# Graph attention layer, one core: units of 128 edges, maxima by a scan, the one-hot transposed through one PSUM bank

## The chip, the cores and the metric

The kernel runs on 1 core of a Trainium2 chip. The metric is the device time of one execution in microseconds (us); what is given is the median of three runs.

## What is computed

One graph attention layer with a residual and a layer norm. There are 6250 nodes of 128 features and 206,250 edges (src, dst), among them one loop per node. Cut to what matters, with recv = src and send = dst, edges sorted by dst:

```python
wn_out = x[send] @ W_lin + b_lin
e_ij = leaky_relu(concat([x[recv], x[send]], -1) @ W_att + b_att, slope=0.2)
a_ij = (e_ij @ w_alpha)[:, 0]
a_exp = exp(a_ij - segment_max(a_ij, recv)[recv])
alpha = a_exp / max(segment_sum(a_exp, recv)[recv], 1e-12)
n_i = segment_sum(alpha[:, None] * wn_out, recv)
out = layernorm(x + elu(n_i))
```

## The kernel before

The nodes are cut into 49 blocks of 128 receivers. A first phase projects every node once: P (the receiver's half of the attention, kept in SBUF as three bf16 parts, `parts_mem`) and a row of 256 values for the sender (Q and V, written to the DRAM table `qv_table`). Meanwhile DVE sorts all edges by receiver block with a bitonic sort of 128 x 2048 keys; the transposes between its runs are PE's, and the copies out of PSUM are ACT's. Padding edges are made by counting (`make_padding`), so that every block fills whole units of `UNIT` = 256 edges. A chunk (`CHUNK`) is 512 edges, `PER` = 2 units; there are `NCH` = 427 chunks, enough for any input of this size.

The main loop runs over the chunks k, on every engine in an order that is written out by hand, with semaphores between the engines. For one chunk:

- ACT copies the senders' numbers (`stage_index`, L515), and POOL issues four indirect DMAs, each of which gathers 128 rows of the table (`gather`, L408 to L418) into one of `U` = 6 places of `rows`. A place is free once the sums of chunk k - 6 are done. After the last chunk four more are gathered (L421).
- DVE compares the lanes (the receivers' numbers within the block) with 0 to 127, which gives a one-hot (`make_onehot`, L954). PE transposes it (`turn_onehot`, L644) into one of two PSUM banks and ACT copies it to SBUF (`copy_onehotT`, L520).
- PE computes the hidden values (`hidden`, L652): per unit three bf16 matmuls of 256 columns, P's parts against the transposed one-hot, and per tile of 128 edges one fp32 matmul of the gathered rows with the identity (two passes each). The stationary operand of the bf16 ones is at an address from a register, the unit's block.
- ACT multiplies by the slope (`slope`, L526), DVE takes the maximum (`leaky_relu`, L961), and PE forms the scores of all 128 receivers for each edge, with a very low number where the receiver is another (`mask`, L670).
- DVE takes each unit's maximum (`lowest`, L975), then for each unit apart the block's new maximum, its growth, and its copy back (`new_peak`, `grow`, `set_peak`). ACT takes the exponential, one instruction per unit, and a factor by which the old sums shrink (`weigh`, L532).
- PE transposes the weights (`turn_weights`, L679), ACT copies them (`copy_weights`, L547), PE multiplies them with the gathered rows into one sum per unit (`chunk_sums`, L687), and DVE adds each unit's sum to its block's (`add_sums`, L1006).

What sets the order around the change is each engine's `step`, which does for several chunks at once:

```python
# PE, step k (L708)
turn_onehot(k + 4, j + 4); chunk_sums(k, j); turn_weights(k + 1, j + 1)
hidden(k + 4, ...); mask(k + 3, j + 3)
# DVE, step k (L1035), without the small operations
lowest(k + 2, j + 2); make_onehot(k + 5, j + 5); leaky_relu(k + 3, j + 3)
add_sums(k, j, 0, now); add_sums(k, j, 1, now)
# ACT, step k (L566)
slope(k + 3); copy_onehotT(k + 4); copy_weights(k + 1); weigh(k + 2); stage_index(k + U + 1)
```

A loop body holds `U` chunks (`chunks`, L295); at its start PE and DVE load the block numbers of its units into registers (`blocks_of`, L307). A tail divides the sums, applies ELU and the layer norm, and stores.

## Time and profile before

| | |
|---|---|
| median of the three runs | 3382.81 us (3382.03 to 3388.4) |
| profiled execution, span from first to last instruction | 2832.4 us |
| profiled execution, its own time | not listed; the median of the runs stands 550.4 us above the span |
| mean granted TensorE clock | 0.989 |
| DVE | 1889.7 us busy, 67%, 6126 instructions |
| ACT | 1479.4 us busy, 52%, 3418 instructions |
| DMA | 241.93 MB, mean 85 GB/s |

The span falls into three parts: sorting and projecting up to the first gather at 511.4 us, the main loop up to about 2779 us, and the tail of 53 us. The page's first part gives busy time by engine, the second the same in 40 slices of 70.8 us; the chain that ended last gives 26% to PE, 23% to DMA, 18% each to DVE and to "issue", 8% to POOL. Lines are lines of the kernel before; PEld is PE's weight load, and "rows<-qv_table,index" is the gather.

### The profile page before, as it was taken

Reading aid. Unit: us, or ns where it says so; the run is one execution under the profiler, and the core shown is the slowest. Engines: PE = TensorE matmul, PEld = TensorE weight load, DVE = VectorE, ACT = ScalarE, POOL = GpSimd, SP = SyncE. Lnnn points to the kernel's source line nnn. Section 1 sums busy time; section 2 is a strip of 40 time slices with the busy share of each in tenths; the row PEclk is TensorE's granted clock in tenths of the full one; section 3 lists DMA queues with packets and bytes.
Section 4 is the critical chain, followed back from the end, with each engine's and each line's share of the span. In section 5 each row is a group of like instructions: output and inputs, shape, how many; then the busy total and the mean of one; then the engine's idle time right before and its main releaser. Section 6 shows DMA issues by size and latency. Waiting matters only on the chain.

```text
span 2832.4 us, 60571 instructions
## 1 busy us (share of the span) xinstructions
PE 2139.7 (76%) x14416; PEld 1626.7 (57%) x14632; DVE 1889.7 (67%) x6126; ACT 1479.4 (52%) x3418; POOL 1725.1 (61%) x1739
## 2 busy tenths in 40 slices
PE   4981111588888888888888888888888888888872
PEld 1321111466666666666666666666766666666651
DVE  7969999666666666666666666666666666666546
ACT  3781111355555555555555555555555555555544
POOL 0000000677777777777777777777777777777760
PEclk9999999999999999999999999999999999999996
DMA  3110000233333333333333333333333333333493
GB/s 98 41 36 2 0 0 0 75 103 100 102 100 101 101 102 101 101 101 101 101 100 101 102 100 102 100 101 101 101 100 100 102 100 101 101 101 101 96 79 63
DMA packets 99135, 241.93 MB, mean 85 GB/s; under 512 B 29041, under 2 KB 42057, under 8 KB 98907
## 3 DMA queue, kind: packets, MB, share of 16 engines
q0 software_dynamic: 82816, 226.19, 29.7%
q1 hardware_dynamic: 16298, 15.51, 1.9%
q8 instruction: 6, 0.10, 0.0%
q14 instruction: 15, 0.12, 0.0%
HBM read 231.91 MB, written 9.68 MB: 85 GB/s over the span
## 4 chain that ended last, share of the span: by engine, by line
PE 26%; DMA 23%; issue 18%; DVE 18%; POOL 8%; DVEq 3%; ACT 3%; SPq 0%; POOLq 0%; ACTq 0%
DMA rows<-qv_table,index 22%; PE hidden_ps L666 9%; POOL rows L415 8%; PE masked_ps L677 8%; DVE keys_i L844 3%; DVE keys_i L843 3%; PE hidden_ps L611 3%; PE hidden_ps L661 3%; PE hidden_ps L610 2%; DVE new_low L990 2%; ACT index L518 1%; DVE onehot L957 1%; DVE leaky L965 1%; DVE growth L998 1%; DVE sums L1013 1%
## 5 line engine op out<-in xcount | busy, mean ns | idle before, releaser
L415 POOL DMA_INDIRECT rows<-qv_table,index x1724 | 1716.7, 996 | 590.1 <-issue 398.8
L980 DVE TENSOR_REDUCE unit_low<-masked_ps 128x2 f32<-128x512 f32 x429 | 296.8, 692 | 797.7 <-PE masked_ps L677 797.7
L666 PE MATMUL hidden_ps<-identf,rows 128*128 128x128 f32 x3448 | 571.8, 289 | 317.7 <-DMA rows<-qv_table,index 317.7
L666 PEld LDWEIGHTS hidden_ps<-identf,rows 128*128 128x128 f32 x3448 | 454.2, 192 | 440.1 <-DMA rows<-qv_table,index 434.9
L693 PE MATMUL turned_ps<-rows,weights 128*128 128x129 f32 x3416 | 475.2, 282 | 0.5 <-ACT weights L551 0.5
L539 ACT ACTIVATE weightsT<-masked_ps,new_low 128x256 f32<-128x256 f32 x858 | 403.8, 471 | 93.3 <-DVE new_low L990 92.2
L677 PE MATMUL masked_ps<-leaky,w_cols 128*128 128x512 f32 x860 | 442.3, 596 | 11.6 <-issue 0.4
L551 ACT ACTIVATE weights<-turned_ps 128x512 f32<-128x512 f32 x428 | 255.5, 597 | 339.2 <-PE turned_ps L684 339.2
L661 PE MATMUL hidden_ps<-onehotT,parts_mem 128*128 128x256 bf16 x2586 | 425.1, 274 | 3.2 <-ACT onehotT L524 3.2
L693 PEld LDWEIGHTS turned_ps<-rows,weights 128*128 128x128 f32 x3416 | 416.2, 192 | 0.6 <-ACT weights L551 0.6
L524 ACT ACTIVATE onehotT<-turned_ps 128x512 bf16<-128x512 bf16 x431 | 257.4, 597 | 304.4 <-PE turned_ps L649 303.8
L530 ACT ACTIVATE sloped<-hidden_ps 128x512 f32<-128x512 f32 x430 | 256.4, 596 | 225.0 <-PE hidden_ps L666 223.3
L1013 DVE SCALAR_TENSOR_TENSOR sums<-sums,shrink,turned_ps 128x129 f32 x854 | 296.0, 347 | 50.1 <-DVE sums L1013 0.2
L965 DVE TENSOR_TENSOR leaky<-hidden_ps,sloped 128x512 f32<-128x512 f32 x430 | 297.4, 692 | 7.0 <-ACT sloped L530 6.9
L649 PEld LDWEIGHTS turned_ps<-identb,onehot 128*128 128x128 bf16 x1724 | 133.1, 98 | 282.7 <-issue 246.0
L957 DVE TENSOR_TENSOR onehot<-lane,lanes 128x512 bf16<-128x512 bf16 x432 | 294.4, 682 | 0.7 <-DVE lanes L948 0.7
L661 PEld LDWEIGHTS hidden_ps<-onehotT,parts_mem 128*128 x2586 | 254.6, 98 | 24.4 <-issue 4.1
L684 PE MATMUL turned_ps<-identf,weightsT 128*128 128x128 f32 x1712 | 256.9, 273 | 0.0
L640 PE MATMUL turned_ps<-identf,keys_i 128*128 128x128 f32 x208 | 51.2, 427 | 230.7 <-DVE keys_i L844 194.1
L684 PEld LDWEIGHTS turned_ps<-identf,weightsT 128*128 128x128 f32 x1712 | 200.7, 141 | 0.5 <-issue 0.5
L649 PE MATMUL turned_ps<-identb,onehot 128*128 128x128 bf16 x1724 | 167.6, 220 | 35.9 <-DVE onehot L957 35.9
L640 PEld LDWEIGHTS turned_ps<-identf,keys_i 128*128 128x128 f32 x208 | 40.8, 223 | 240.9 <-DVE keys_i L844 165.1
(123 smaller groups left out, 1984.9 us busy)
## 6 DMA issues: line engine op xcount, KB each, us to landing
rows<-qv_table,index POOLq DMA_INDIRECT x1724
qv_table<-qv_out SPq DMA_DIRECT2D x49, 128.0 KB, 1.7
out<-x_sb SPq DMA_DIRECT2D x2, 1344.0 KB
keys_i<-in_src SPq DMA_DIRECT2D x1, 768.0 KB
keys_i<-in_dst SPq DMA_DIRECT2D x1, 768.0 KB
recv<-in_src SPq DMA_DIRECT2D x1, 604.5 KB
out<-x_sb SPq DMA_DIRECT2D x1, 256.0 KB
recv<-in_src SPq DMA_DIRECT2D x1, 195.2 KB
```

Of the source, the lines that this page charges most:

```text
L415: g.indirect_dma_start(out=rows[:, j, c, 0:2 * F], out_offset=None, in_=table, in_offset=bass.IndirectOffsetOnAxis(ap=index[:, j, c:c + 1] ...
L539: last = a.activation(weightsT[:, j % 2, unit], masked_ps[:, j % 2, unit], ACT.Exp, bias=new_low[:, j % 2, i:i + 1])
L649: mm = t.transpose(onehotT_ps[:, j % 2, c * P:(c + 1) * P], onehot[:, j % 2, c, :], identb[:])
L661: t.matmul(whole[:, unit], p_parts[:, bass.ds(of[i], 1), s, :].rearrange("p a f -> p (a f)"), onehotT[:, j % 3, unit], start=(s == 0), sto ...
L666: mm = t.matmul(whole[:, c * P:(c + 1) * P], rows[:, j % U, c, 0:F], identf[:], start=False, stop=(c == (i + 1) * UC - 1), skip_group_chec ...
L677: t.matmul(whole, w_cols[:], leaky[:, j % 2, :], start=False, stop=True).then_inc(masked_done, 1)
L684: mm = t.transpose(weights_ps[:, c * P:(c + 1) * P], weightsT[:, j % 2, c * P:(c + 1) * P], identf[:])
L693: mm = t.matmul(unit_sums_ps[:, c // UC, :], weights[:, j % 2, c * P:(c + 1) * P], rows[:, j % U, c, F:R], start=(c % UC == 0), stop=(c % ...
L957: v.tensor_tensor(onehot[:, j % 2], lane[:].unsqueeze(1).to_broadcast([P, C, P]), lanes[:, bass.ds(k * C, C)].unsqueeze(2).to_broadcast([P ...
L965: v.tensor_tensor(leaky[:, j % 2, :], hidden_ps[:, j % 2, :], sloped[:, j % 2, :], ALU.max).then_inc(leaky_ready, 1)
L980: v.tensor_reduce(unit_low[:], masked_ps[:, j % 2, :].rearrange("p (i e) -> p i e", i=PER), AX_X, ALU.max, negate=True).then_inc(unit_low_ ...
L1013: v.scalar_tensor_tensor(out=at, in0=at, scalar=shrink[:, j % 2, i:i + 1], in1=unit_sums_ps[:, i, :], op0=ALU.mult, op1=ALU.add).then_inc( ...
```

## The change

- `UNIT` is 128 edges (`PER` = 4), so a chunk holds four units, one per tile; with less padding `NCH` is 415. Nothing is gathered after the last chunk, and no step issues work for a chunk past it (`real`).
- The ring of gathered rows has 8 places (`U`); a loop body holds 8 chunks and loads block numbers every 4 (`HALF`).
- The running maxima of a chunk's units come from one scan: a table `fresh` (made once, in the sort) holds a high number where a unit is the first of its block, and `peaks` keeps the maximum after every unit. Growth is one subtraction per chunk.
- In `hidden` the gathered rows are transposed (one pass) ahead of P's parts, which are matmuls of 128 columns; the wait for the gather is the first of the stage.
- The transposed one-hot has one PSUM bank in place of two, and four places in SBUF. PE transposes it for chunk k + 5 in step k. The bank gained goes to the sums, which have one region per unit.
- ACT's step is ordered anew; the exponentials are of 128 columns.
- Lanes and senders stay in the sorted layout and are read with a stride. The sort has one more stage. Several buffers share memory.

```diff
-    PER = 2
+    PER = 4
...
-    SLOTS = 8
+    SLOTS = 14
     AHEAD = 4
-    U = 6
+    U = 8
+    HALF = U // 2
...
+    assert BODIES * U + AHEAD < NCH
...
-        onehotT_ps = turned_ps[:, 0:2 * CHUNK].bitcast(BF16).rearrange("p (s c) -> p s c", s=2)
-        weights_ps = turned_ps[:, 2 * CHUNK:3 * CHUNK]
-        sums_ps = turned_ps[:, 3 * CHUNK:4 * CHUNK]
+        onehotT_ps = turned_ps[:, 0:CHUNK].bitcast(BF16)
+        weights_ps = turned_ps[:, CHUNK:2 * CHUNK]
+        unit_sums_ps = turned_ps[:, 2 * CHUNK:4 * CHUNK].rearrange("p (i c) -> p i c", i=PER)[:, :, 0:F + 1]
...
             chunks(pool, gather)
-            for k in range(NCH, NCH + AHEAD):
-                gather(k // U, k % U)
...
             def weigh(k, j):
...
+                act.wait_ge(new_low_ready, k + 1)
                 for i in range(PER):
                     unit = slice(i * UNIT, (i + 1) * UNIT)
-                    act.wait_ge(new_low_ready, k * PER + i + 1)
                     last = a.activation(weightsT[:, j % 2, unit], masked_ps[:, j % 2, unit], ACT.Exp,
-                                        bias=new_low[:, j % 2, i:i + 1])
+                                        bias=peaks[:, bass.ds(k * PER + i + 1, 1)])
...
             def step(i, j):
                 k = i * U + j
-                slope(k + 3, j + 3)
-                copy_onehotT(k + 4, j + 4)
-                copy_weights(k + 1, j + 1)
-                weigh(k + 2, j + 2)
-                stage_index(k + U + 1, (j + 1) % U, i + 1 + (j + 1) // U)
+                if real(k + 5):
+                    copy_onehotT(k + 5, j + 5)
+                if real(k + 2):
+                    weigh(k + 2, j + 2)
+                if real(k + 1):
+                    copy_weights(k + 1, j + 1)
+                if real(k + 4):
+                    slope(k + 4, j + 4)
+                if real(k + U + 1):
+                    stage_index(i, j + U + 1)
...
             def turn_onehot(k, j):
                 pe.wait_ge(onehot_ready, k + 1)
-                if past(k, 2):
-                    pe.wait_ge(onehotT_ready, k - 1)
+                if past(k, 1):
+                    pe.wait_ge(onehotT_ready, k)
...
             def hidden(k, j, rounds, of):
                 pe.wait_ge(onehotT_ready, k + 1)
                 if past(k, 2):
                     pe.wait_ge(leaky_ready, k - 1)
+                pe.wait_ge(gathered[j % U], rounds * (16 * C))
                 whole = hidden_ps[:, j % 2, :]
                 for i in range(PER):
                     unit = slice(i * UNIT, (i + 1) * UNIT)
+                    t.matmul(whole[:, unit], rows[:, j % U, i, 0:F], identf[:], is_transpose=True,
+                             start=True, stop=False, skip_group_check=True)
                     for s in range(3):
-                        t.matmul(whole[:, unit], p_parts[:, bass.ds(of[i], 1), s, :].rearrange("p a f -> p (a f)"),
-                                 onehotT[:, j % 3, unit], start=(s == 0), stop=False, skip_group_check=True)
-                    if i == 0:
-                        pe.wait_ge(gathered[j % U], rounds * (16 * C))
-                    for c in range(i * UC, (i + 1) * UC):
-                        mm = t.matmul(whole[:, c * P:(c + 1) * P], rows[:, j % U, c, 0:F], identf[:],
-                                      start=False, stop=(c == (i + 1) * UC - 1), skip_group_check=True)
+                        mm = t.matmul(whole[:, unit], p_parts[:, bass.ds(of[i], 1), s, :].rearrange("p a f -> p (a f)"),
+                                      onehotT[:, j % 4, unit], start=False, stop=(s == 2), skip_group_check=True)
...
             def step(i, j, ahead):
                 k = i * U + j
-                turn_onehot(k + 4, j + 4)
+                if real(k + 5):
+                    turn_onehot(k + 5, j + 5)
                 chunk_sums(k, j)
-                turn_weights(k + 1, j + 1)
-                hidden(k + 4, j + 4, i + 1 + (j + 4) // U, ahead[j * PER:(j + 1) * PER])
-                mask(k + 3, j + 3)
+                if real(k + 1):
+                    turn_weights(k + 1, j + 1)
+                if real(k + 4):
+                    hidden(k + 4, j + 4, i + 1 + (j + 4) // U, ahead)
+                if real(k + 3):
+                    mask(k + 3, j + 3)
...
+            def new_peaks(k, j):
+                dve.wait_ge(unit_low_ready, k + 1)
+                if past(k, 1):
+                    dve.wait_ge(new_low_ready, k)
+                v.tensor_tensor_scan(peaks[:, bass.ds(k * PER + 1, PER)], fresh[:, bass.ds(k * PER, PER)], unit_low[:],
+                                     peaks[:, bass.ds(k * PER, 1)], ALU.max, ALU.min).then_inc(new_low_ready, 1)
...
             def step(i, j, of):
                 k = i * U + j
-                lowest(k + 2, j + 2)
-                make_onehot(k + 5, j + 5)
...
-                leaky_relu(k + 3, j + 3)
...
+                if real(k + 2):
+                    lowest(k + 2, j + 2)
+                    new_peaks(k + 2, j + 2)
+                if real(k + 5):
+                    make_onehot(i, j + 5)
+                if real(k + 3):
+                    leaky_relu(k + 3, j + 3)
+                if real(k + 2):
+                    old_peaks(k + 2, j + 2)
+                    mark_ones(i, j + 2)
+                    grow(k + 2, j + 2)
+                for n in range(PER):
+                    add_sums(k, j, n, of)
```

How the change moves instructions, at three places. First, PE at the start of the main loop's lead-in. `onehot` is what DVE made, `turned_ps` the PSUM it is transposed into; before:

```order
L310 TENSOR_LOAD blocks [waits w_cols_ready,split,blk_loaded]
L649 MATMUL turned_ps<-identb,onehot 128x128 [waits onehot_ready]
L649 MATMUL turned_ps<-identb,onehot 128x128 x3
L661 ISA [waits onehotT_ready]
L661 MATMUL hidden_ps<-onehotT,parts_mem 128x256
```

and now:

```order
L297 TENSOR_LOAD blocks [waits w_cols_ready,split,blk_loaded]
L646 MATMUL turned_ps<-identb,onehot 128x128 [waits onehot_ready]
L646 MATMUL turned_ps<-identb,onehot 128x128 x3
L646 MATMUL turned_ps<-identb,onehot 128x128 [waits onehotT_ready,onehot_ready]
L646 MATMUL turned_ps<-identb,onehot 128x128 x3
L658 MATMUL hidden_ps<-identf,rows 128x128 [waits gathered0,onehotT_ready]
```

One transpose of four tiles more stands ahead of the first hidden stage: PE is one one-hot further on than before, and stays so in the loop.

Second, DVE's step for one chunk in the loop. `unit_low` are the units' maxima (negated), `low_peak` or `peaks` the running ones; before:

```order
L980 TENSOR_REDUCE unit_low<-masked_ps 128x2 [waits new_low_ready,masked_done]
L957 TENSOR_TENSOR onehot<-lane,lanes 128x512 [waits onehotT_done]
L990 ISA [waits peak_ready,weightsT_ready,unit_low_ready]
L990 TENSOR_TENSOR new_low<-unit_low,low_peak 128x1
L972 TENSOR_SCALAR rows<-lanes 128x4 [waits chunk_sums_done]
L998 TENSOR_TENSOR growth<-new_low,low_peak 128x1 [waits shrink_ready,new_low_ready]
L965 TENSOR_TENSOR leaky<-hidden_ps,sloped 128x512 [waits masked_done,sloped_ready]
```

and now:

```order
L986 TENSOR_REDUCE unit_low<-masked_ps 128x4 [waits new_low_ready,masked_done]
L994 SCALAR_TENSOR_TENSOR peaks<-fresh,peaks,unit_low 128x4 [waits new_low_ready,unit_low_ready]
L961 TENSOR_TENSOR onehot<-lane,lanes 128x512 [waits onehotT_done]
L969 TENSOR_TENSOR leaky<-hidden_ps,keys_i 128x512 [waits masked_done,sloped_ready]
L1002 TENSOR_TENSOR old_low<-peaks,fresh 128x4 [waits growth_ready,new_low_ready]
```

The one-hot stands behind the reduction as before, and now behind the scan as well, which waits for the reduction.

Third, PE's step in the loop, from the weights' transposes into the hidden stage; before:

```order
L684 MATMUL turned_ps<-identf,weightsT 128x128 [waits weights_ready,weightsT_ready]
L684 MATMUL turned_ps<-identf,weightsT 128x128 x3
L661 ISA [waits leaky_ready,onehotT_ready]
L661 MATMUL hidden_ps<-onehotT,parts_mem 128x256
L661 ISA
L661 MATMUL hidden_ps<-onehotT,parts_mem 128x256
```

and now:

```order
L679 MATMUL turned_ps<-identf,keys_i 128x128 [waits weights_ready,weightsT_ready]
L679 MATMUL turned_ps<-identf,keys_i 128x128 x3
L658 MATMUL hidden_ps<-identf,rows 128x128 [waits gathered5,leaky_ready,onehotT_ready]
L661 ISA
L661 MATMUL hidden_ps<-onehotT,parts_mem 128x128
```

The wait for the gather moved ahead of P's matmuls. Each of these, an ISA row (a register computation) and a matmul, is half as wide and comes twelve times per chunk in place of six.

## Rows read from the trace of the kernel before

**Rows 1.** The page, parts 1 and 2: busy time; busy tenths of POOL in 40 slices.

```profile
PE 2139.7 (76%) x14416; PEld 1626.7 (57%) x14632; DVE 1889.7 (67%) x6126; ACT 1479.4 (52%) x3418; POOL 1725.1 (61%) x1739
...
POOL 0000000677777777777777777777777777777760
```

**Rows 2.** All instructions of line 415, POOL's gathers, and what its idle time ended with.

```profile
L415 POOL DMA_INDIRECT rows<-qv_table,index x1724: 942/946/2342, 511.4 to 2768.4; - x192
...
  issue: 398.8, 1273
```

**Rows 3.** The timeline of POOL: start, us, instruction, [idle before, releaser].

```profile
1202.48 0.95 POOL L415 DMA_INDIRECT rows<-qv_table,index  x1 [0.30 <-issue]
1203.73 1.32 POOL L415 DMA_INDIRECT rows<-qv_table,index  x1 [0.30 <-issue]
1205.36 0.94 POOL L415 DMA_INDIRECT rows<-qv_table,index  x1 [0.31 <-issue]
```

**Rows 4.** Two stretches: length, busy us (instructions) of each engine, granted clock, DMA.

```profile
540.00:2660.00 2120.00, 1822.13 (x13263) 1449.22 (x13466) 1317.19 (x4893) 1212.67 (x2857) 1623.19 (x1632) 1.00 0.35 101
2660.00:2769.00 109.00, 81.41 (x560) 64.33 (x568) 55.76 (x208) 50.35 (x120) 70.12 (x73) 0.95 0.84 82
```

**Rows 5.** The timeline of PE over one chunk.

```profile
1201.57 0.38 PE L676 MATMUL masked_ps<-onehotT,other 128*128 128x512 bf16 x1
1201.79 1.02 PE L677 MATMUL masked_ps<-leaky,w_cols 128*128 128x512 f32 x2
1202.65 0.39 PE L649 MATMUL turned_ps<-identb,onehot 128*128 128x128 bf16 x4
1202.87 1.11 PE L693 MATMUL turned_ps<-rows,weights 128*128 128x129 f32 x8
1203.82 0.60 PE L684 MATMUL turned_ps<-identf,weightsT 128*128 128x128 f32 x4
1204.25 0.49 PE L661 MATMUL hidden_ps<-onehotT,parts_mem 128*128 128x256 bf16 x3
1205.30 0.71 PE L666 MATMUL hidden_ps<-identf,rows 128*128 128x128 f32 x4 [0.56 <-DMA rows<-qv_table,index]
```

**Rows 6.** The timeline of DVE over the same chunk.

```profile
1202.94 0.69 DVE L980 TENSOR_REDUCE unit_low<-masked_ps 128x2 f32<-128x512 f32 x1 [1.99 <-PE masked_ps L677]
1203.55 0.68 DVE L957 TENSOR_TENSOR onehot<-lane,lanes 128x512 bf16<-128x512 bf16 x1
```

**Rows 7.** The timeline of all engines where the pipeline fills.

```profile
520.24 1.29 DVE L957 TENSOR_TENSOR onehot<-lane,lanes 128x512 bf16<-128x512 bf16 x2 [0.68 <-DVE lanes L948]
...
520.99 0.61 PE L649 MATMUL turned_ps<-identb,onehot 128*128 128x128 bf16 x4 [35.94 <-DVE onehot L957]
...
529.96 0.68 DVE L980 TENSOR_REDUCE unit_low<-masked_ps 128x2 f32<-128x512 f32 x1
...
530.78 0.16 DVE L990 TENSOR_TENSOR new_low<-unit_low,low_peak 128x1 f32<-128x1 f32 x1
```

**Rows 8.** The updates of the sums (line 1013) and DVE's register loads (line 310).

```profile
L1013 DVE SCALAR_TENSOR_TENSOR sums<-sums,shrink,turned_ps x854: 341/348/353, 540.5 to 2778.9; 128x129 f32 x171
...
L310 DVEq TENSOR_LOAD <-blocks x73: 597/1101/1128, 519.6 to 2771.0; - x73
```

**Rows 9.** PE after its longest wait of the even stretch, and the clock granted behind it.

```profile
1975.72 0.71 PE L666 MATMUL hidden_ps<-identf,rows 128*128 128x128 f32 x4 [2.03 <-DMA rows<-qv_table,index]
...
1977.20:1980.40 3.20, 2.98 (x11) 1.89 (x11) 0.91 (x2) 1.18 (x2) 2.45 (x3) 0.50 0.44 123
```

**Rows 10.** The timeline of DVE: the last stage of the sort.

```profile
507.50 1.23 DVE L843 TENSOR_TENSOR keys_i<-keys_i 128x1024 f32<-128x1024 f32 x1
508.64 1.22 DVE L844 TENSOR_TENSOR keys_i<-keys_i 128x1024 f32<-128x1024 f32 x1
```

More of the change, by code:

```diff
@@ L675, in mask @@
                 whole = masked_ps[:, j % 2, :]
-                t.matmul(whole, other[:], onehotT[:, j % 3, :], start=True, stop=False)
+                t.matmul(whole, other[:], onehotT[:, j % 4, :], start=True, stop=False)
                 t.matmul(whole, w_cols[:], leaky[:, j % 2, :], start=False, stop=True).then_inc(masked_done, 1)
@@ L1046, in step @@
-                new_peak(k + 2, j + 2, 1, later)
-                add_sums(k, j, 1, now)
-                grow(k + 2, j + 2, 1, later)
-                set_peak(k + 2, j + 2, 1, later)
-            chunks(dve, step, lambda i: blocks_of(mybir.EngineType.DVE, i, 0, U + 2))
+                if real(k + 2):
[5 more added lines that the diff above has]
+                    leaky_relu(k + 3, j + 3)
```

233 lines of the change are left out of this document (116 added, 117 removed).

## Prediction

> **What bounds the kernel now.** The page first [rows 1]: PE is the busiest engine (76%), POOL is at 61% and gathers from slice 8 to slice 38 without a break; no engine is full. A busy share cannot choose between them, so the next view is POOL's own line. The 1724 gathers are four for each chunk of 512 edges (427 chunks and 4 after them), 0.946 us in the median, and nearly all of POOL's idle time is put down to "issue" or to a releaser of a moment ago [rows 2]. The timeline shows why: each gather starts 0.30 us after the end of the one before, whatever the releaser's name, and now and then one takes 1.32 us in place of 0.95, beside the one-hot comparison on DVE, which starts 0.18 us before it [rows 3, 6]. So a chunk costs POOL 4 x 0.946 + 4 x 0.305 + about 0.2 = 5.2 us, and POOL never truly waits. In the long even stretch it was busy 1623 of 2120 us, with 1632 gathers: 1.30 us for each, 5.20 us a chunk, at full TensorE clock [rows 4]. The others follow it: PE stands before the matmuls that use gathered rows (the row at 1205.30) [rows 5], DVE waits 1.99 us before the reduction over the masked scores [rows 6]. **POOL's gathers are the bound, and PE and DVE each have about a microsecond of slack per chunk.** After the last edge the chunks hold nothing but padding; in 2660 to 2769 us 73 gathers take 109 us, 1.49 us each [rows 4].
>
> **What goes with fewer chunks.** 427 + 4 gathered chunks become 415 with none after them. If POOL stayed the bound, 16 chunks at 5.2 us would go, 83 us.
>
> **What the PE work of a chunk becomes.** Differences of starts give what the work holds PE for [rows 5]: four bf16 transposes of the one-hot 0.22 us (1202.65 to 1202.87), the eight passes of the sums 0.95, four fp32 transposes of the weights 0.43, the bf16 mask 0.22, and the fp32 mask matmuls 1.02 to their end. In the hidden stage the eight fp32 passes of the gathered rows become four transposes, priced like those of the weights: 0.43. Six matmuls of 256 columns become twelve of 128. Their nearest row at 128 bf16 columns is the one-hot's, four weight loads with four matmuls in 0.22 us, 0.055 each: 0.67 us. The bound on the other side is the 256-column row, 0.49 us for three with 0.16 of it tail, so 0.11 each: 1.32. I take 0.055, because load, type and columns are the same, and keep the other end. From the first one-hot transpose to the end of the mask: 0.22 + 0.95 + 0.43 + 0.43 + 0.67 + 0.22 + 1.02 = **3.94 us**. PE has less work than before.
>
> The Trainium skill, TensorE: Matmul & The Clock Gate, section Back-to-back issue gap, says that a sustained stream of weight load and matmul pairs runs at about 81 ns a pair for 128 columns. The row of this trace says 55 ns for four pairs; by the page's figure an estimate for the twelve is 1.0 us in place of 0.67.
>
> **The step in which the slack goes.** In the loop before, PE's step k transposes one-hot k+4, and DVE's step k makes one-hot k+5: it lies ready a whole step ahead. After, PE's step k starts with the transposes of one-hot k+5, and DVE still makes k+5 in its step k. DVE makes it behind the reduction and the scan for chunk k+2, and the reduction waits for the mask of k+2, which is the last work of PE's step k-1. So nothing overlaps on this path: PE's whole step, then reduction, scan, one-hot, then PE's whole next step. That circle bounds the chunk, whatever the engines' busy shares are:
> - end of the mask to the start of the reduction: 1201.79 + 1.02 to 1202.94, 0.13 us [rows 5, 6]; the floor is 0.04;
> - reduction 0.69 [rows 6];
> - hand-over to an instruction that needs it at once: 529.96 + 0.68 to 530.78, 0.14 [rows 7];
> - the scan over four columns, which the trace does not show: between the 0.16 us of the one-column minimum [rows 7] and 0.3; I take 0.16, since its four columns are far nearer to one than to the hundreds of a long operation;
> - one-hot 0.68 [rows 6], and to PE's first transpose 520.24 + 0.69 to 520.99, 0.06 [rows 7]. DVE may prepare the one-hot during the scan, so no further gap;
> - PE's step 3.94.
>
> Sum: 0.13 + 0.69 + 0.14 + 0.16 + 0.68 + 0.06 + 3.94 = **5.80 us**, above POOL's 5.20. POOL gets ahead until its ring of eight is full, then waits.
>
> **What else can lie on it.** DVE's four updates of the sums (0.348 us each) [rows 8] take the place of two. Each waits for the one before; with the 0.14 hand-over they need 1.96 us. They start once the sums' matmuls end, 0.22 + 1.11 us into PE's step, and end at about 3.3, before the mask does at 3.94: covered, by 0.6 us. The block numbers are loaded into registers every four chunks in place of six, 1.10 us on DVE's sequencer [rows 8]. The load begins once the last update is handed over, near 3.0, and ends near 4.1, about when the next reduction may start: 0 to 0.4 us late in one chunk of four; I take 0.05 a chunk. The three small operations per unit (minimum, growth, copy) become two per chunk: they hung on nothing and save nothing now. ACT's two exponentials of 256 columns become four of 128; ACT was busy 1213 of 2120 us [rows 4], 2.97 a chunk, and stays under 4: covered by the circle's 5.8, and also worth nothing if POOL is the bound. But its order matters: it now copies the weights after the shrink factor, which waits for the updates; 3.3 + 0.2 + 0.6 = 4.1 us, needed at 3.94 + 1.86 + 0.22 = 6.0. Covered.
>
> **TensorE's clock.** PE now stands still for the circle's DVE part, 1.86 us, in every chunk. In the long stretch before, where PE paused for less, the clock was granted in full [rows 4]; but after one wait of 2.03 us for a gather it was granted at 0.50, the 1.2 GHz level, in 1977.2 to 1980.4 us [rows 9]. Work on PE takes twice as long there, so such a fall costs about half of these 3.2 us. With pauses nearly as long as that wait in every chunk, I take one fall in eleven chunks, 0.15 a chunk; its ends are 0 and the rival below. Together 5.80 + 0.05 + 0.15 = **6.0 us a chunk**.
>
> **The sum.** The updates ran from 540.5 to 2778.9 us [rows 8], with the last one's end 2779.3. After: 410 full steps at 6.0 = 2460; the last five issue no hidden stage, about 3.7 each, 18. The sorting phase gets one more stage over 2048 keys, 2.4 us [rows 10], a table of 1792 columns in three operations, at those rows' price 2 us each, and loses wider padding and a strided unpacking; I take +1, between -6 and +6. So the last update ends at 540.5 + 1 + 2460 + 18 = 3019.5, 240 us later. The 53 us behind it stay. The profiled execution has a span of 2832.4 us; the median of the runs is 3382.8, and the 550.4 us between them are in no view. I keep them constant: 2832.4 + 240 = 3072 in the profile, and **3382.8 + 240 = 3623 us**. Low end of this case: 5.6 a chunk (all hand-overs at their floors, no load, no fall), 3459. High end: 6.5, 3828.
>
> **Rivals.**
> - *The short matmul pairs are slow.* Each of the twelve is preceded by a register computation; if pairs with one run at 0.08 to 0.11 us, the circle grows by 0.3 to 0.66 us: 410 of these are 123 to 271 us, **3746 to 3894**. For it: the 256-column rows never show a shorter pace, as they can't. 
> - *The clock falls regularly.* If the 1.86 us pause takes the clock to 1.2 GHz in every second chunk, at 1.6 us each, a chunk costs 0.65 us more than forecast, 267 us in 410: **3890**, and twice that if it does so in every chunk. For it: [rows 9]. Against: PE is busy for two thirds of the chunk. Chance 0.12.
> - *POOL stays the bound*, the side of faster. Its place is the gather, its price 5.2 us a chunk, and it decides once the circle is shorter than POOL's period. Then 83 us go, **3300**. This needs the circle 0.6 us shorter than its own rows; or a gather that is dearer in the timed runs than in the profile: if the 550 us outside the span lay in the 1724 gathers, 0.32 us each, POOL's period would be 6.5 and cover the circle's 6.0, and 16 chunks fewer would save 100 us. Nothing in the trace speaks for it. Chance 0.12.
> - *The one-hot is not on a circle*, because some step ahead hides it: the order of both engines, with one more transpose in PE's lead-in but as many one-hots in DVE's, excludes it. It would end as the rival before; its chance is in there.
>
> **How the numbers follow.** Forecast 0.58, slow pairs 0.18, clock 0.12, POOL 0.12. The time is the forecast's, 3623. The range takes in the forecast's ends and the slow pairs: 3450 to 3900; outside are POOL's case and the worse half of the clock's. A change of 0.2%, 7 us, is about what a measurement of this kernel can tell from none. Faster 0.12, within it 0.02 (the POOL case with a circle just over it), slower 0.86.
>
> **What would show it.** In the profile after: gathers with idle time before them that ends with the sums' matmuls; DVE's one-hot followed within 0.1 us by PE's transposes, which wait on it each chunk; the reduction waiting for the mask, less than 4 us of PE work between; a chunk period of 5.7 to 6.4; the twelve pairs in about 0.7 us. It is wrong if the gathers still follow each other at 1.30 us, if one-hots lie ready before PE asks, or if the span grows by less than 75 us; if the span goes as said and the time does not, what lies outside the span was no constant.

## The result, and the profile after

| | median of the runs |
|---|---|
| before | 3382.42 us (3378.69 to 3388.4, 4 runs) |
| after | 3647.11 us (3634.74 to 3658.77, 4 runs; granted clock 0.814 to 0.855) |

The ratio is 1.0787, 95% interval 1.0758 to 1.0816: slower by 264.7 us, where 3623 (+240) was predicted. The kernel before takes about 3382 us in some sessions on a chip and 2834 in others (both on one and the same chip, ten minutes apart), and the rows ahead of the prediction come from an execution of the second kind, while the measured ratio comes from the first. So each ratio below is taken to the kernel before of its own session. What differs between the sessions is a subject of the experiments.

The profiled execution of the changed kernel took 3643.12 us with a span of 3641.1: 2 us apart, not 550. Its page, first and second part:

```profile
span 3641.1 us, 65506 instructions
...
PE 2307.6 (63%) x14980; PEld 1770.6 (49%) x14981; DVE 2113.6 (58%) x5544; ACT 1417.7 (39%) x4145; POOL 1608.8 (44%) x1675
...
POOL 0000034555555554555555555555555555555550
PEclk9985557888888887888888888888888887888886
```

POOL, which had no real pause before [rows 1], is down to 44%, and the mean granted clock is near 0.8 in nearly every slice of the loop. The gathers and the updates of the sums, each from the view of its line (count, duration min/median/max, first and last start), and the longest waits of the kernel (us in total, times, longest):

```profile
L408 POOL DMA_INDIRECT rows<-qv_table,index x1660: 943/949/2057, 515.4 to 3549.1; - x185
...
L1020 DVE SCALAR_TENSOR_TENSOR sums<-sums,shrink,turned_ps x1660: 348/349/353, 571.5 to 3587.8; 128x129 f32 x185
```

```profile
POOL rows L408 <- PE turned_ps L688: 924.6, 332, 14.8
...
PE turned_ps L646 <- DVE onehot L961: 751.6, 303, 34.0
...
DVE unit_low L986 <- PE masked_ps L672: 433.5, 340, 3.0
```

A gather costs what it did [rows 2], but now POOL waits for its ring (L688 are the sums' matmuls). PE waits for the one-hot, and DVE for the mask: the circle of the prediction, with its names. From the first update to the last it is 3016.3 us for 415 chunks, 7.27 each. The timeline of two chunks, PE and the three DVE operations of the circle (start, duration, in brackets the idle time before and who ended it):

```profile
1501.33 0.44 PE L646 MATMUL turned_ps<-identb,onehot 128*128 128x128 bf16 x4 [2.13 <-DVE onehot L961]
1501.86 1.15 PE L688 MATMUL turned_ps<-rows,keys_i 128*128 128x129 f32 x8
1502.85 0.60 PE L679 MATMUL turned_ps<-identf,keys_i 128*128 128x128 f32 x4
1503.28 0.27 PE L658 MATMUL hidden_ps<-identf,rows 128*128 128x128 f32 x1
1503.39 0.33 PE L661 MATMUL hidden_ps<-onehotT,parts_mem 128*128 128x128 bf16 x3
1503.56 0.28 PE L658 MATMUL hidden_ps<-identf,rows 128*128 128x128 f32 x1
...
1504.63 1.02 PE L672 MATMUL masked_ps<-leaky,w_cols 128*128 128x512 f32 x2
1505.68 0.69 DVE L986 TENSOR_REDUCE unit_low<-masked_ps 128x4 f32<-128x512 f32 x1 [0.70 <-PE masked_ps L672]
1506.63 0.23 DVE L994 TENSOR_TENSOR_SCAN peaks<-fresh,peaks,unit_low 128x4 f32 x1 [0.26 <-issue]
1506.85 0.69 DVE L961 TENSOR_TENSOR onehot<-lane,lanes 128x512 bf16<-128x512 bf16 x1
1507.59 0.40 PE L646 MATMUL turned_ps<-identb,onehot 128*128 128x128 bf16 x4 [1.95 <-issue]
1507.83 1.96 PE L688 MATMUL turned_ps<-rows,keys_i 128*128 128x129 f32 x8
1509.58 1.06 PE L679 MATMUL turned_ps<-identf,keys_i 128*128 128x128 f32 x4
```

PE does the work of the first chunk at full clock, 6.26 us from transpose to transpose. In the second the same eight passes of the sums take 1.96 us in place of 1.15 and the transposes 1.06 in place of 0.60: the 1.2 GHz level, after a pause of 1.95 us. The next L646 starts at 1515.17, 7.58 us later.

Taking the differences between the starts of successive one-hot transposes over the whole loop, 134 chunks hold no time at the low level, with a median of 5.94 us; 278 hold some, with a median of 7.58. (The ends of the mask show where the difference lies: the median from the one-hot's transpose to there, PE's step, is 3.99 us in the first kind and 5.63 in the second.) By windows the granted clock is even (PE, PEld, DVE, ACT and POOL busy with counts, then clock, DMA share, GB/s); 273 gathers in 500 us are 7.33 us a chunk:

```profile
1500.00:2000.00 500.00, 351.72 (x2387) 282.35 (x2388) 265.99 (x754) 198.87 (x613) 263.00 (x273) 0.83 0.25 72
```

### The profile page after: what moved, and what is told of

Read it like the earlier page. It is cut to its first block, busy times and chain, and to the rows that moved or that the text cites. A ratio compares the mean times of both kernels' runs of the same rounds, so it can differ in the third digit from the quotient of the medians.

```text
span 3641.1 us, 65506 instructions
## 1 busy us (share of the span) xinstructions
PE 2307.6 (63%) x14980; PEld 1770.6 (49%) x14981; DVE 2113.6 (58%) x5544; ACT 1417.7 (39%) x4145; POOL 1608.8 (44%) x1675
## 4 chain that ended last, share of the span: by engine, by line
PE 54%; DVE 22%; issue 14%; DVEq 4%; another core or an unknown queue 3%; ACT 1%; DMA 1%; SPq 0%; ACTq 0%
PE turned_ps L688 16%; PE masked_ps L672 8%; PE hidden_ps L661 8%; PE turned_ps L679 6%; DVE onehot L961 6%; PE hidden_ps L658 5%; DVE unit_low L986 5%; PE turned_ps L646 5%; DVE sums L1020 3%; DVE keys_i L854 3%; DVE keys_i L853 3%; PE hidden_ps L608 2%; PE masked_ps L671 2%; PE hidden_ps L607 2%
## 5 line engine op out<-in xcount | busy, mean ns | idle before, releaser
L408 POOL DMA_INDIRECT rows<-qv_table,index x1660 | 1600.4, 964 | 1486.0 <-PE turned_ps L688 924.6
L1020 DVE SCALAR_TENSOR_TENSOR sums<-sums,shrink,turned_ps 128x129 f32 x1660 | 580.2, 350 | 702.8 <-PE turned_ps L688 489.5
L646 PE MATMUL turned_ps<-identb,onehot 128*128 128x128 bf16 x1660 | 184.1, 240 | 969.3 <-DVE onehot L961 751.6
L646 PEld LDWEIGHTS turned_ps<-identb,onehot 128*128 128x128 bf16 x1660 | 104.0, 103 | 1311.2 <-DVE onehot L961 809.5
L986 DVE TENSOR_REDUCE unit_low<-masked_ps 128x4 f32<-128x512 f32 x415 | 287.0, 692 | 613.9 <-PE masked_ps L672 433.5
L688 PE MATMUL turned_ps<-rows,keys_i 128*128 128x129 f32 x3320 | 627.4, 348 | 8.4 <-ACT keys_i L539 6.4
L661 PE MATMUL hidden_ps<-onehotT,parts_mem 128*128 128x128 bf16 x4980 | 617.9, 250 | 0.3 <-issue 0.3
L688 PEld LDWEIGHTS turned_ps<-rows,keys_i 128*128 128x128 f32 x3320 | 540.7, 246 | 20.4 <-ACT keys_i L539 11.0
L661 PEld LDWEIGHTS hidden_ps<-onehotT,parts_mem 128*128 x4980 | 519.5, 119 | 51.9
L527 ACT ACTIVATE keys_i<-masked_ps,peaks 128x128 f32<-128x128 f32 x1660 | 472.1, 375 | 2.7 <-DVE peaks L994 2.7
L679 PE MATMUL turned_ps<-identf,keys_i 128*128 128x128 f32 x1660 | 356.7, 356 | 0.0
L969 DVE TENSOR_TENSOR leaky<-hidden_ps,keys_i 128x512 f32<-128x512 f32 x415 | 283.7, 684 | 35.6 <-issue 34.2
L679 PEld LDWEIGHTS turned_ps<-identf,keys_i 128*128 128x128 f32 x1660 | 289.0, 191 | 1.1 <-issue 0.6
L637 PE MATMUL turned_ps<-identf,keys_i 128*128 128x128 f32 x208 | 50.3, 422 | 231.7 <-DVE keys_i L854 195.1
```

The costliest lines, as they stand in the source:

```text
L408: g.indirect_dma_start(out=rows[:, j, c, 0:2 * F], out_offset=None, in_=table, in_offset=bass.IndirectOffsetOnAxis(ap=index[:, j, c:c + 1] ...
L527: last = a.activation(weightsT[:, j % 2, unit], masked_ps[:, j % 2, unit], ACT.Exp, bias=peaks[:, bass.ds(k * PER + i + 1, 1)])
L646: mm = t.transpose(onehotT_ps[:, c * P:(c + 1) * P], onehot[:, j % 2, c, :], identb[:])
L661: mm = t.matmul(whole[:, unit], p_parts[:, bass.ds(of[i], 1), s, :].rearrange("p a f -> p (a f)"), onehotT[:, j % 4, unit], start=False, s ...
L679: mm = t.transpose(weights_ps[:, c * P:(c + 1) * P], weightsT[:, j % 2, c * P:(c + 1) * P], identf[:])
L688: mm = t.matmul(unit_sums_ps[:, c, :], weights[:, j % 2, c * P:(c + 1) * P], rows[:, j % U, c, F:R], start=True, stop=True)
```

## The experiments

### First session: what costs the changed kernel its time, and the kernel before again

e1 is the kernel before, unchanged.

> The kernel before, unchanged, to see its span and granted clock in every run. The changed kernel's span lies 2 us under its time, so the 550 us between time and span of the kernel before are no constant. Theory A (its timed runs run in another regime than its one profiled execution: the short pauses of TensorE at the gathered rows let the clock fall, as they did once in the trace): time near 3382 us, span near 3380, granted clock 0.80 to 0.90. Theory B (something outside the span of this kernel alone): span near 2832, clock 0.99, time near 3382.

Measured: 3384.32 us, ratio 1.0005 (0.9995 to 1.0015), span 3384.1. The span is as long as the time, so the 550 us are inside it: the first update starts 14 us later than in the rows ahead of the prediction (554.2 against 540.5), and from the first update to the last it is 2776 us in place of 2238. **538 of the 550 us are in the main loop.** That is the outcome that theory A expected; its cause, the clock, is another matter. The window of 1500 to 2500 us, and its longest waits:

```profile
1500.00:2500.00 1000.00, 764.47 (x5091) 606.12 (x5089) 497.76 (x1848) 422.54 (x1077) 603.28 (x615) 0.88 0.28 81
```

```profile
DVE unit_low L980 <- remote: 669.2, 103, 7.8
...
ACT weights L551 <- remote: 509.0, 178, 7.9
...
ACT sloped L530 <- remote: 355.7, 100, 10.9
```

615 gathers in 1000 us: 6.50 us a chunk, not 5.2 [rows 4]. ACT's L551 copies the weights and L530 multiplies by the slope. "Remote" is what the profile says when no instruction on the core ended close to the release. One such place in the timeline, PE, ACT and DVE:

```profile
1505.62 0.60 PE L684 MATMUL turned_ps<-identf,weightsT 128*128 128x128 f32 x4
...
1507.82 1.02 PE L677 MATMUL masked_ps<-leaky,w_cols 128*128 128x512 f32 x2
1508.67 0.39 PE L649 MATMUL turned_ps<-identb,onehot 128*128 128x128 bf16 x4
...
1511.01 0.60 ACT L551 ACTIVATE weights<-turned_ps 128x512 f32<-128x512 f32 x1 [5.29 <-remote]
...
1511.74 1.15 PE L693 MATMUL turned_ps<-rows,weights 128*128 128x129 f32 x8 [2.68 <-issue]
...
1515.34 0.60 ACT L530 ACTIVATE sloped<-hidden_ps 128x512 f32<-128x512 f32 x1 [2.81 <-remote]
1515.48 0.69 DVE L980 TENSOR_REDUCE unit_low<-masked_ps 128x2 f32<-128x512 f32 x1 [7.40 <-remote]
```

ACT's copy L551 waits for the transposes L684, which are over at 1506.2, and starts at 1511.01. DVE's reduction waits for the mask L677, over at 1508.84, and starts at 1515.48. The trace's records of the semaphores agree: the signals of L684 and L677 are there at 1510.98 and 1515.37. **PE's completion signals come late**. Long waits like these two are met about once in 26 us (103 for DVE's reduction), but smaller delays are common: in the loop the signal of L684 comes more than 0.5 us after the end of its matmul in 296 of its 424 records, the latest by 7.7 us. Signals of DVE and ACT follow the end of their instruction within 0.02 us wherever they are recorded. In the trace ahead of the prediction no signal of PE in the loop is late by more than 0.02 us. Between the long waits PE runs chunk after chunk in 4.23 us, so POOL's bound of 5.2 is undershot and then given back.

The changed kernel has them too, but in its loop they are fewer (the hidden stage's signal is over 0.5 us late in 40 of 414 records). One ahead of it is long. Where the pipeline fills and gathers follow each other without a pause, the hidden stage's last matmul ends at 531.59 and its signal stands at 555.88, and all wait for it:

```profile
531.07 0.53 PE L661 MATMUL hidden_ps<-onehotT,parts_mem 128*128 128x128 bf16 x3
...
555.91 0.60 ACT L518 ACTIVATE keys_i<-hidden_ps 128x512 f32<-128x512 f32 x1 [26.77 <-remote]
```

e2 takes the one-hot off the circle: DVE makes it one chunk earlier.

```diff
             make_onehot(0, 0)
+            make_onehot(0, 1)
             for k in range(4):
-                make_onehot(0, k + 1)
+                make_onehot(0, k + 2)
...
-                if real(k + 5):
-                    make_onehot(i, j + 5)
+                if real(k + 6):
+                    make_onehot(i, j + 6)
```

> The changed kernel, but DVE makes one-hot k+6 in step k (and one more in its lead-in), so that it lies ready a step before PE transposes it. Theory A (the circle of PE's whole step with reduction, scan and one-hot bounds the chunk, and the pause in it lets the clock fall): the circle is broken, POOL's 5.2 us bound again, 541 + 415 x 5.25 + 53 = 2770 us, at most 2900, clock over 0.97. Theory B (DVE's longer step with four updates is the bound by itself): 5.8 to 6.3 us a chunk, 3000 to 3200 us. Theory C (the regime of the clock is what the kernel before suffers too): 3200 to 3400 us.

Measured: 3352.74 us, ratio 0.9903 (0.9883 to 0.9923). That is 8% below the changed kernel and 1% below the kernel before, so **the one-hot's place is what made the change slower than the kernel before**. But the 2770 us expected of theory A were missed by far, and the time is in the range of theory C, where both kernels suffer from the same thing. The loop stays at 6.6 us a chunk:

```profile
1500.00:2500.00 1000.00, 747.15 (x5287) 561.71 (x5288) 581.27 (x1663) 438.71 (x1363) 592.54 (x606) 0.86 0.28 79
```

Chunks without low clock take 5.23 us here, POOL's period; those with it take 8.16, and the late signals are here too:

```profile
DVE unit_low L986 <- remote: 592.7, 112, 6.9
```

e3 leaves the one-hot for k + 5 but puts it first in DVE's step:

```diff
+                if real(k + 5):
+                    make_onehot(i, j + 5)
                 if real(k + 2):
                     lowest(k + 2, j + 2)
                     new_peaks(k + 2, j + 2)
-                if real(k + 5):
-                    make_onehot(i, j + 5)
```

> The changed kernel, but DVE makes one-hot k+5 at the start of its step, ahead of the reduction and the scan. Theory A: PE can start its step after DVE's last update and a 0.7 us one-hot, while the reduction still waits for nothing but the mask; the one-hot is off the circle, 5.2 to 5.5 us a chunk, 2750 to 2880 us if the clock stays up. Theory B (DVE's work is the bound): no better than 6 us a chunk, 3080 us.

Measured: 3419.68 us, ratio 1.0104 (1.0085 to 1.0124). The two swapped blocks are worth 227 us. The expected 2750 to 2880 were missed as in e2: the 203 chunks without low clock have a median of 5.09 us, as theory A said, but those with it 6.84, and the mean is 6.8.

e4 fills PE's pause in the changed kernel with matmuls that nobody reads, after the mask:

```diff
+            def idle_work(k, n):
+                pe.wait_ge(onehotT_ready, k)
+                for _ in range(n):
+                    t.matmul(turned_ps[:, 256:256 + P], identb[:], identb[:], start=True, stop=True)
...
                     mask(k + 3, j + 3)
+                if real(k + 5):
+                    idle_work(k + 6, 16)
```

> The changed kernel with 16 small matmuls after the mask, identity against identity into unused columns of the one-hot's bank, about 0.9 us of work in PE's pause of 1.9 us; nothing waits for them. Their result is read by nobody. Theory A (1.03 of the 7.33 us of a chunk are the clock, which falls because of the pause): the clock stays over 0.97 and the chunk takes the circle's 6.26 us: 541 + 410 x 6.26 + 18 + 53 = 3180 us. Rival (the pause is not what lowers the clock): clock near 0.82 and time 3640 us or more.

Measured: 3513.9 us, ratio 1.0392 (1.0365 to 1.042): 133 us less, with more work on PE and the same circle.

```profile
1500.00:2500.00 1000.00, 762.64 (x7327) 638.41 (x7328) 553.19 (x1579) 417.20 (x1288) 562.31 (x572) 0.93 0.26 75
```

The clock is at 0.93 in place of 0.83. The time at the low level between 600 and 3300 us fell from 870 to 365 us. So PE's own pause lets the clock fall, and the fall costs time. The expected 3180 was missed by far: PE is still 1 us idle after the filler, 137 chunks still hold low clock, and the late signals have become more (that of the one-hot's transposes is over 0.5 us late in 249 of 387 records, in the changed kernel in none of the 249 that are recorded).

### Second session: where the late signals come from

e5 puts the same 16 matmuls into e2, e8 puts them into the kernel before, after its mask. e7 leaves out two of P's three parts in e2's hidden stage (`for s in range(1)`). In e6 three of a chunk's four gathers are left out. The scaled exponential and the larger divisor only keep the numbers bounded, since most gathered rows are then stale and the output means nothing:

```diff
-                for c in range(C):
+                for c in range(1 if past(k, U) else C):
                     g.indirect_dma_start(
...
-                    act.wait_ge(gathered[r], rounds * (16 * C))
+                    act.wait_ge(gathered[r], rounds * 16 + 48)
...
-                a.activation(shrink[:, j % 2, :], growth[:, j % 2, :], ACT.Exp).then_inc(shrink_ready, 1)
+                a.activation(shrink[:, j % 2, :], growth[:, j % 2, :], ACT.Exp, scale=0.0).then_inc(shrink_ready, 1)
...
-                pe.wait_ge(gathered[j % U], rounds * (16 * C))
+                pe.wait_ge(gathered[j % U], rounds * 16 + 48)
...
-            v.tensor_scalar(recip[:], sums[:, :, F], 1e-12, None, ALU.max).then_inc(finish, 1)
+            v.tensor_scalar(recip[:], sums[:, :, F], 100.0, None, ALU.max).then_inc(finish, 1)
```

> e2_ahead (the changed kernel with the one-hot made one chunk earlier) with 16 more bf16 matmuls of 128 columns per chunk on PE after the mask, which nobody reads. In e2_ahead the lowest 29 percent of the time lies at 1.2 GHz, and about once in 26 us PE's completion signals reach the other engines 4 to 7 us late. Theory A (the pauses cost through the clock): the low share falls as in e4_filler, from 29 to under 15 percent, and the time falls from 3353 to 3200 to 3280 us. Theory B (the late signals are the cost, and each PE instruction adds to them): 32 more PE instructions per chunk make them longer or more frequent, 3450 to 3600 us. Theory C (late signals come after long stretches of PE without a pause, whatever it does): 3400 us or more.

> e2_ahead where, after the first eight chunks, only the first of a chunk's four tiles of 128 rows is gathered (three of four gathers are left out, so those rows are stale; the factor by which old sums shrink is 1, and the divisor at the end is at least 100). POOL's work falls from 5.0 to 1.3 us per chunk and the gathers' traffic to a quarter. Theory D (the late signals of PE come from the gathers' traffic or from POOL's descriptors): they vanish, the loop runs at PE's step of 4.3 us, and the time is 2500 to 2700 us. Theory B (they come from the number of PE's own instructions): they stay, and the loop keeps 6.0 to 6.6 us per chunk, 3150 to 3350 us. A mean of 5.0 to 5.5 us per chunk (2850 to 3000 us) would say that both take part.

> e2_ahead with one of P's three bf16 parts in the hidden values instead of three (the two smaller parts are left out, so the scores are less exact): 8 of 36 pairs of weight load and matmul per chunk are gone, PE's step is 0.45 us shorter. Theory B (late signals follow the number of PE's instructions): they become at least a quarter rarer or shorter; e2_ahead's 6.6 us per chunk fall to 5.5 to 5.9, 2900 to 3050 us. Theory D (traffic of the gathers): no fewer, 3250 to 3350 us. Theory C (long stretches without a pause): PE now pauses in every chunk under POOL's 5.2 us, so they vanish and the loop runs at 5.2 to 5.4 us, 2800 to 2880 us.

> The kernel before with 16 more bf16 matmuls of 128 columns per chunk on PE after the mask, in unused columns of a one-hot's bank, which nobody reads. PE's step grows from 4.2 to 5.1 us, just under POOL's 5.2. Theory A (clock): the low share falls from 24 percent to under 12, the time from 3383 to 3200 to 3300 us. Theory B (number of PE's instructions): 3500 to 3700 us. Theory C (stretches without a pause): 3450 us or more.

| beside a kernel before of 3380.89 us | us | ratio (95%) | us a chunk, first to last gather |
|---|---|---|---|
| e5, e2 with filler | 3437.02 | 1.0158 (1.0134 to 1.0182) | 6.82 |
| e6, e2 with a quarter of the gathers | 2696.9 | 0.7977 (0.7964 to 0.7991) | 5.0 |
| e7, e2 with 8 of 35 pairs fewer on PE | 3343.77 | 0.9892 (0.9874 to 0.9909) | 6.57 |
| e8, before with filler | 3475.04 | 1.0279 (1.0261 to 1.0297) | 6.73 |

e7 speaks against theories B and C: 8 fewer of the 35 pairs on PE (its expectation says 36) change the period by 0.05 us against e2 of the session before, where B expected 5.5 to 5.9 and C 5.2 to 5.4. Theory D holds: with a quarter of the gathers DVE's reduction waits for "remote" once, for 5.7 us, in place of 112 times, and the clock stays full. And e6 shows it within one execution. In the first eight chunks, which still gather all four tiles, a signal of the hidden stage is 26 us late (its matmul ends at 537.45, the signal stands at 563.54); after 600 us none of PE's is more than 0.54 us late.

The period of e6 is 5.0 us and not the 4.3 that theory D expected, so the 2696.9 us are only just in its range. What bounds it is a second circle, which the prediction had as covered under the longer one. ACT makes the shrink factor only after the updates of the sums and copies the weights after that, and PE's next sums wait for the copy, 414 times (e6's window, then its waits):

```profile
1500.00:2500.00 1000.00, 814.56 (x7000) 639.72 (x6999) 765.98 (x2200) 564.01 (x1800) 197.69 (x200) 1.00 0.09 26
...
ACT shrink L533 <- DVE sums L1020: 828.2, 413, 2.5
...
PE turned_ps L688 <- ACT keys_i L539: 369.6, 414, 3.2
```

e5 and e8 are the point of interest for theory A, which expected them below 3300 us. In e8 the clock goes to 0.98 and time at the low level all but vanishes (72 us between 600 and 3300), and still the kernel is 94 us slower (e8's window, then its longest wait):

```profile
1500.00:2500.00 1000.00, 809.36 (x7258) 665.03 (x7256) 481.03 (x1778) 389.53 (x1036) 592.46 (x593) 0.98 0.27 78
...
ACT onehotT L524 <- remote: 1205.2, 392, 4.2
```

So a loop of this kernel can be held above 6.5 us a chunk by late signals alone, at nearly full clock. In the kernel before and in e2 the low clock is then most likely a follower of the pauses that late signals make. What it costs there on top was not measured, because the filler changes both: with it the signal of the one-hot's transposes is over 0.5 us late in 401 of 431 records, without it (e1) in 198 of 367. More instructions on PE made the signals later, fewer (e7) did not help. In these two sessions every kernel that gathers four tiles a chunk and could do it in under 6.5 us ends between 6.5 and 6.8.

### Third session: bytes or number, and each kernel's own circle

e9 fetches half rows in e2 (after the first eight chunks):

```diff
+                    wide = F if past(k, U) else 2 * F
                     g.indirect_dma_start(
-                        out=rows[:, j, c, 0:2 * F], out_offset=None, in_=table,
+                        out=rows[:, j, c, 0:wide], out_offset=None,
+                        in_=table if wide == 2 * F else table.rearrange("r (h f) -> (r h) f", h=2),
...
-                             ACT.Copy).then_inc(indexed, 1)
+                             ACT.Copy, scale=2.0 if past(k, U) else 1.0).then_inc(indexed, 1)
```

e10, e11 and e12 have e6's edit: two of four gathers in e2, one of four in the changed kernel, one of four in the kernel before.

> e2_ahead where, after the first eight chunks, each of the four gathers of a chunk fetches 128 half rows (512 bytes instead of 1 KB; the V half of the row is stale, and the divisor at the end is at least 100). Same number of gathers and of completion signals, half the bytes. Theory D1 (what makes PE's signals late is the bytes that the gathers move): like half of the gathers, 5.0 to 5.6 us per chunk, 2700 to 2930 us. Theory D2 (it is the number of gathers, with their descriptors and the 16 completion signals of each): no change, 6.4 to 6.7 us per chunk, 3260 to 3370 us.

> e2_ahead with two of four gathers per chunk after the first eight chunks (the other two tiles' rows are stale; shrink factor 1, divisor at least 100): the bytes of e9_ahead_halfrows with half the number of gathers. D1 and D2 both expect late signals to be few: between e6_ahead_quarter's 2697 and 2850 us. If the time were above 3100, neither bytes nor number would be it, but something that any two gathers in a row do.

> The changed kernel itself with one of four gathers per chunk after the first eight chunks (otherwise as e6_ahead_quarter). Theory A1 (the clock's falls in the changed kernel come from the pause of about 2 us that its own circle of waits puts into each chunk): the falls stay, about one in two chunks, and the period is 7.0 to 7.3 us, 3500 to 3640 us. Theory A2 (the falls come from the late signals alone): clock near 1, the circle at full clock of 6.26 us per chunk, less 0.05 for what the gathers' signals cost, 3180 to 3230 us. By the prediction's own sum (5.80 us of circle and 0.05 of register loads) it would be 3020 to 3050 us.

> The kernel before with one of four gathers per chunk after the first six chunks (otherwise as e6_ahead_quarter). Theory D (late signals of PE, made by the gathers, cost the kernel before its difference to 5.2 us per chunk, and POOL the rest): without them it runs at PE's step of 4.2 us or DVE's 4.2, 540 + 431 x 4.3 + 70 = 2430 to 2560 us. If the time stays above 2900 us, the difference between 5.2 and 6.5 us per chunk has another source in the kernel before than in e2_ahead.

In the third session the kernel before took 2833.76 us (2832.73 to 2834.76, 7 runs), on the chip of the second session, and no kernel shows a late signal.

| beside a kernel before of 2833.76 us | us | ratio (95%) | us a chunk, mean between one-hot transposes |
|---|---|---|---|
| e9, e2 with half rows | 2717.7 | 0.9592 (0.9576 to 0.9608) | 5.10 |
| e10, e2 with two of four gathers | 2670.85 | 0.9424 (0.9408 to 0.944) | 4.99 |
| e11, after with a quarter of the gathers | 3575.33 | 1.2619 (1.2597 to 1.264) | 7.2 |
| e12, before with a quarter | 2418.03 | 0.8533 (0.8518 to 0.8547) | 4.28 |

e9 and e10 were to tell D1 from D2 and can't: without late signals in the session, neither bytes nor number had anything to act on. That question stays open. What they give is something else: e9 has all four gathers and runs at POOL's 5.1 us, with the circle through ACT, which sets e10's 4.99, close behind. e12 shows that PE's step, 4.23 us, is the kernel before's next bound (PE is busy for 788 of 800 us); its 2418 us are a little under the expected 2430 to 2560, as e10's 2671 are under 2697.

e11 is the clean measurement of what the prediction argued about: no late signals, a quarter of the gathers, and it is nearly as slow as with all of them. Beside it e10, with more gathers and the one-hot one chunk earlier, takes 904 us less in the same session; this pair is the strongest evidence for the circle. Its window, and a chunk at full clock with the DVE work after it:

```profile
1500.00:2000.00 500.00, 354.93 (x2380) 287.01 (x2415) 265.94 (x758) 201.57 (x619) 65.19 (x69) 0.82 0.06 18
```

```profile
1508.55 0.40 PE L646 MATMUL turned_ps<-identb,onehot 128*128 128x128 bf16 x4 [1.95 <-DVE onehot L961]
1508.78 1.12 PE L688 MATMUL turned_ps<-rows,keys_i 128*128 128x129 f32 x8
...
1511.52 1.02 PE L672 MATMUL masked_ps<-leaky,w_cols 128*128 128x512 f32 x2
```

From 1508.55 to 1511.52 + 1.02 is PE's step: 3.99 us. 112 chunks without low clock have a median of 5.94 us, 301 with some have 7.57, in all 7.20. Theory A1 holds: with no late signal in the loop and few gathers, the pauses of the circle are enough to bring the clock down, and about three chunks in four hold some of the low level.

## Why the prediction was right, and where only its sum was

The sign and the cause were right. That the time was right is luck: two large errors of the sum cancelled. In the profile 3072 us were predicted and 3641 came, 569 more. Outside the span 550 us were taken as constant, and 2 came, 548 fewer. What is left is 20 us of 3643. The step that failed first is "I keep them constant": the kernel before's own 3382 us are a loop of 6.5 us a chunk, as e1 shows, and the changed kernel at 7.3 is slow enough that late signals add little to it (0.10 us a chunk against e11). One sentence of the rivals came close, a gather dearer in the timed runs, "POOL's period would be 6.5". The period was 6.5, but the gathers are not dearer (median 0.949 us) and POOL is not the one that is late.

- **The circle, 5.80 and with the register loads 5.85**: 5.94 in the median of chunks at full clock, both in the changed kernel and in e11. PE's step was 3.94 predicted, 3.99 in e11. The twelve short pairs run at about 0.056 us: 1503.39 to 1503.56 for three. The Trainium skill's 81 ns (TensorE: Matmul & The Clock Gate, Back-to-back issue gap) are not what this trace shows, and the rival of slow pairs is out. The scan took 0.23 us and not 0.16, the hand-over to it 0.26 and not 0.14; the reduction starts 0.03 us after the mask's end and not 0.13.
- **The clock, 0.15 a chunk**: this term was mis-sized, and no row had given its one fall in eleven chunks. Its rival, "the clock falls regularly", had the price right (1.6 us; 7.57 - 5.94 = 1.63 measured) and put it at one chunk in two, 0.65 more than forecast. (Its "twice that" for every chunk should have been 1.45 a chunk, 595 us.) e11 shows 301 of 413 chunks with low clock. From its first update to its last it is 2974 us, where the sum has 2478: 496 of the 569 us. The circle's 5.94 for 5.85 makes some 37 of them, the clock the other 459: about 1.25 us a chunk in place of 0.15. "PE is busy for two thirds of the chunk" was no argument against it.
- **The rest of the 569**: the first update starts at 571.5 and not 541.5. Of these 30 us 25 are the late signal at 531.59, since e11, which has none, starts at 546.1; the other 5 are the sort and the lead-in. The last 43 are the loop itself, 3016 us against e11's 2974: what late signals and the full gathers add to the changed kernel.
- **The gathers no longer the bound, the ring full**: right, 924.6 us of POOL's waits. The four updates are 0.49 us apart and covered, as said.
- **The range** held the time, but for the same mixed reason. For a session without late signals, e11 says at least about 3575 us against 2834, +26%, where the sum for the profile said 3072. The changed kernel with all its gathers was not run in such a session.

A version that beats both kernels is e2: 0.9903 of before and 0.92 of after where signals are late. Where they aren't, it was not run; only e9 stands for it: 0.9592, with half rows.

## What to carry to other kernels

When a program-ordered pipeline is rearranged, walk the circle once: if what an engine makes in step k is needed first in the other's step k + 1 and itself hangs on the other's last work of step k, the steps add up, and a single slot more of distance is worth more than the operations saved (here 294 us where signals are late, against 12 chunks fewer). The circle's 1.9 us of idle TensorE in each chunk had a second price, half the clock for part of the next, and it was the larger one here: 1.2 us a chunk, where the circle itself is 0.7 above POOL's 5.2. And never carry a gap between a profile's span and the timed runs through a sum: first get a profile of an execution that took the time of the runs.

## What the runs showed of the hardware

- PE's completion signals can be late while matmuls go on issuing at their usual pace, by up to 7.7 us in e1's loop and by 24 us (the changed kernel) and 26 us (e6) where the pipeline fills, in one session and not in the next on the same chip. They come with the traffic of gathers: in e6 they all but vanish once only one gather in four is left. 8 of 35 pairs fewer on PE did not help (e7), 16 more made them more frequent (e8). In such sessions the trace of a kernel with all its gathers also lacks many semaphore records (1624 of 4584 are there for one gather semaphore in e1), while without late signals nearly all are there.
- The Trainium skill (NOTIFIC — the notification-queue block, Overflow: three behaviours, one of which stalls the engine) says that the block which takes up such records always pushes back on its producers when its inner queues are full, and that a stall counter above zero would mean that it had slowed an engine. No run here shows whether the recording or the gathers' own signals hold PE's back. It fits only in part: PE itself goes on, and records are missing, which by the same section happens when the queue's memory is full. If recording is the cause, the late signals are a matter of the measurement and not of the kernel; that stays open.
- With pauses of 1.9 us, each between 4 us of dense work, 301 of 413 chunks hold time at the 1.2 GHz level (e11), and the mean clock is 0.81. In e6, e10 and e12, whose pauses are shorter, it falls at most once between 600 and 2500 us.
- Sixteen matmuls without a purpose made the changed kernel 3.7% faster (e4), and the kernel before 2.8% slower (e8).
